# Graph layer on one core: v repeated through DRAM instead of on TensorE, and G of the next block in front of the sums over units

## The chip, the cores and the metric

One Trainium2 chip, one of its cores. The metric is device time in microseconds of one execution. The kernel before takes 751.27 us (median of 3 runs, 750.43 to 751.88).

## What is computed

A message-passing step over 53125 edges (25000 drawn pairs in both directions and 3125 loops, sorted by destination) of 3125 nodes with 32 features each (8 scalars and 8 vectors), then a layer norm. Cut to what matters:

```python
r = edge_vec / norm(edge_vec);  sh1 = SQRT3 * r
xs, xd = x[edge_src], x[edge_dst]
s1, v1 = scalars and vectors of (xs, xd)                       # 16 + 16x3 per edge
w  = relu(emb @ fc1_w1 / sqrt(10)) @ fc1_w2 / sqrt(16)         # 512 weights per edge
s_t, v_t = a1 * (sums over the 16 units of s1, v1 with w)      # "the first tensor product"
w2 = relu(emb @ fc2_w1 / sqrt(10)) @ fc2_w2 / sqrt(16)         # 384 weights per edge
scal, gates, vecs = a2 * (sums over the 8 units of s_t, v_t with w2)
edge_out = concat(tanh(scal), vecs * tanh(gates)) * edge_weight
out = layernorm(x + segment_sum(edge_out, edge_dst))
```

The per-edge weights are never formed. Instead the features are multiplied by the constant second matrices (G), the product is multiplied by the hidden layer (p), and the sum over hidden units is a matmul (S1); the second tensor product is done in the same way (z, then S2).

## The kernel before

Edges go in NB = 104 blocks of 512 (four tiles of 128). Every engine has its program written out by hand as a loop over steps i; in a step each engine works on several blocks at once, and the order of the calls in a step is the order in its queue. Semaphores with counts tie the engines; each result waits for the one that it needs and for the reader of what it overwrites. PSUM is one tensor `ps` of eight banks, shared as the code fixes it.

The stages of a block m, with the function and the line of the profile:

- GpSimd gathers the source rows (L362), TensorE turns the destinations' places into one-hot matrices (`spread_places` L921, `spread_edges` L937) and picks the destination rows out of a window (`rows` L1007). ScalarE copies all of them to SBUF. GpSimd multiplies by the directions (L404, L405), VectorE sums along them (`sum_along` L764), TensorE transposes the features (`turn_features` L947), ScalarE copies them (f, L483).
- G: `first_layer` (L1039), four f32 products (eight passes) into banks 0 to 3. `hidden_1` (L1026) gives the first hidden layer in bank 5; ScalarE applies relu (h1, L523).
- p: `products` on VectorE (L732), p_s = banks 0 to 3 times h1, 128 x 2048.
- S1: `sum_1` (L959), the sum over units of p_s into bank 7: v. ScalarE copies v to bf16 (`part_of_v` L517), TensorE takes that copy off in PSUM by the matrices `less` (`less_part` L966), and so twice more: v ends as three bf16 parts. `repeat` (L995) spreads the parts by `rep_m` over all 128 partitions into banks 0 to 3.
- z: `products2` (L770), banks 0 to 3 times the second hidden layer (h2, relu on ScalarE L529, from `hidden_2` L1032 in bank 6), 128 x 2048. S2: `sum_2` (L977) into bank 5. ScalarE copies it (u, L489), TensorE transposes u (`turn` L1019) into bank 7.
- VectorE: `gates` (L781, L784, L786) read the transposed u, then `gate_sums` (L790, L793), tanh on ScalarE (L471), `gated` (L752), `outputs` (L757). TensorE sums over nodes with the one-hot matrix (`over_nodes` L987), VectorE adds the strip of nodes into `acc` (`accumulate` L745).

On VectorE a step is: p of block i, gates of i-3, z of i-1, gated of i-4, accumulate of i-5, gate sums of i-3, outputs of i-4, sum along of i+2. SyncE's queue loads the windows, the edges' embeddings (three copies of 30 KB per block) and, every 12 blocks, the next group of embeddings. In front of the loop stands a fill that loads the inputs, splits x and the embeddings into three bf16 parts, stores these to DRAM (`x_dram`, `e_dram`) and makes the constants; behind it the last blocks are drained and the layer norm is done.

## Time and profile before

| what | us |
|---|---|
| median of the runs | 751.27 |
| profiled execution, its own time | 750.24 |
| span of the profiled execution | 748.4 |
| PE (TensorE matmul) busy | 690.1 |
| DVE (VectorE) busy | 691.3 |
| ACT (ScalarE) busy | 558.7 |
| POOL (GpSimd) busy | 529.2 |
| p, first start to last start | 38.0 to 714.7 |

The mean granted TensorE clock is 0.991 of full speed. PEld is TensorE's weight load, which overlaps its matmuls. In the chain of work that ended last, PE has 86% of the span and DVE 5%. A name such as `ps<-f,w_f` tells output and inputs of an instruction; "x4" that four rows are merged into one; `[0.19 <-PE ps L1039]` that the engine was idle for 0.19 us before it, until that one released it. The starts in a timeline are measured, the ends of matmuls modelled.

### The profile page before, as it was taken

How to read it: one execution, taken by the hardware profiler on the slowest of the kernel's cores; microseconds unless marked ns; L12 is line 12 of the kernel's file. 1: busy time of each engine (PE TensorE's matmuls, PEld its weight loads, DVE VectorE, ACT ScalarE, POOL GpSimd, SP SyncE). 2: the span in 40 equal slices, each digit the busy share in tenths (PEclk: the TensorE clock that was granted, in tenths of full speed). 3: DMA queues.
4: the chain of work that ended last, by engine and by line, in shares of the span. 5: the costliest groups of instructions: out<-in, count | busy, mean ns of one | idle time of the engine just before them, and what ended most of it. 6: DMA issues, size and time to landing. Idle time of an engine off the chain costs nothing.

```text
span 748.4 us, 19329 instructions
## 1 busy us (share of the span) xinstructions
PE 690.1 (92%) x5998; PEld 285.0 (38%) x5998; DVE 691.3 (92%) x1230; ACT 558.7 (75%) x1279; POOL 529.2 (71%) x656
## 2 busy tenths in 40 slices
PE   0578999999999999999999999999999999999963
PEld 0323434444443443444444344444444444444321
DVE  7578999999999999999999999999999999999983
ACT  2257778887788888877888888888888878788741
POOL 5678787778876887688768876888688877886100
PEclk9999999999999999999999999999999999999997
DMA  4332211121111111121112111211121111111000
GB/s 111 77 91 48 44 31 29 40 46 27 28 42 45 31 28 43 26 46 29 42 26 48 31 42 25 45 29 44 26 48 29 31 36 37 28 27 28 12 1 23
DMA packets 45714, 28.49 MB, mean 38 GB/s; under 512 B 23191, under 2 KB 43833, under 8 KB 45613
## 3 DMA queue, kind: packets, MB, share of 16 engines
q1 hardware_dynamic: 31175, 19.22, 9.8%
q0 software_dynamic: 13312, 6.84, 6.2%
q10 hardware_dynamic: 1126, 1.18, 0.6%
q8 instruction: 52, 0.85, 0.5%
q14 instruction: 49, 0.40, 0.2%
HBM read 22.46 MB, written 4.74 MB: 36 GB/s over the span
## 4 chain that ended last, share of the span: by engine, by line
PE 86%; DVE 5%; issue 2%; ACT 1%; DMA 1%; POOL 0%; DVEq 0%; ACTq 0%
PE ps L1039 15%; PE ps L959 14%; PE ps L977 13%; PE ps L966 9%; PE ps L1019 8%; PE ps L947 6%; PE ps L995 5%; PE ps L1032 4%; PE ps L1026 3%; PE ps L937 3%; DVE p_s L732 3%; PE ps L1007 3%; PE ps L921 2%; PE ps L987 2%; DVE z_s L770 1%
## 5 line engine op out<-in xcount | busy, mean ns | idle before, releaser
L362 POOL DMA_INDIRECT xs<-in_xp,src_i x416 | 401.7, 966 | 114.2 <-issue 104.1
L732 DVE TENSOR_TENSOR p_s<-ps,h 128x2048 f32<-128x2048 f32 x104 | 238.2, 2291 | 20.7 <-PE ps L1039 19.1
L770 DVE TENSOR_TENSOR z_s<-ps,h 128x2048 f32<-128x2048 f32 x104 | 237.6, 2284 | 1.0 <-PE ps L995 1.0
L517 ACT CAST v_s<-ps 128x512 bf16<-128x512 f32 x312 | 182.3, 584 | 48.7 <-PE ps L959 43.6
L1039 PE MATMUL ps<-f,w_f 32*128 32x512 f32 x832 | 120.4, 646 | 4.3
L977 PE MATMUL ps<-z_s,w_z 128*32 128x512 f32 x832 | 110.8, 605 | 2.5 <-DVE z_s L770 2.5
L959 PE MATMUL ps<-p_s,sum_m 128*32 128x512 f32 x832 | 111.8, 606 | 0.2
L483 ACT COPY f<-ps 128x512 f32<-128x512 f32 x104 | 60.9, 586 | 41.8 <-PE ps L947 41.8
L966 PE MATMUL ps<-v_s,less 128*128 128x512 bf16 x208 | 81.1, 390 | 2.3 <-ACT v_s L517 2.1
L1019 PEld LDWEIGHTS ps<-ident,u 128*128 128x128 f32 x416 | 43.8, 141 | 86.7 <-issue 86.7
L523 ACT ACTIVATE h<-ps 128x512 f32<-128x512 f32 x104 | 62.1, 597 | 19.7 <-PE ps L1026 12.4
L404 POOL TENSOR_TENSOR along<-fe,r 128x192 f32<-128x192 f32 x104 | 54.1, 520 | 30.7 <-ACT fe L495 29.3
L489 ACT COPY u<-ps 128x512 f32<-128x512 f32 x104 | 61.2, 588 | 12.4 <-PE ps L977 1.9
L529 ACT ACTIVATE h<-ps 128x512 f32<-128x512 f32 x104 | 62.2, 598 | 10.6 <-PE ps L1032 5.5
L1019 PE MATMUL ps<-ident,u 128*128 128x128 f32 x416 | 68.0, 286 | 0.2
L477 ACT ACTIVATE oht<-ps 126x512 bf16<-126x512 f32 x104 | 62.5, 601 | 7.5 <-PE ps L921 1.5
L947 PE MATMUL ps<-ident,fe 128*128 128x128 f32 x416 | 63.5, 276 | 2.9 <-ACT ohs L512 2.8
L921 PE MATMUL ps<-place,spread 5*126 5x512 bf16 x104 | 40.3, 387 | 16.7 <-DMA place<-place_dram 16.7
L966 PEld LDWEIGHTS ps<-v_s,less 128*128 128x128 bf16 x208 | 19.9, 96 | 89.4 <-ACT v_s L517 76.9
L405 POOL TENSOR_TENSOR fe<-fe,r 128x192 f32<-128x192 f32 x104 | 53.7, 517 | 0.0
L987 PEld LDWEIGHTS ps<-ohs,eo_all 128*32 128x32 f32 x832 | 25.3, 108 | 69.1 <-issue 66.4
L947 PEld LDWEIGHTS ps<-ident,fe 128*128 128x128 f32 x416 | 49.2, 143 | 5.7 <-issue 5.2
(129 smaller groups left out, 847.4 us busy)
## 6 DMA issues: line engine op xcount, KB each, us to landing
emb<-e_dram SPq DMA_DIRECT2D x309, 30.0 KB
xs<-in_xp,src_i POOLq DMA_INDIRECT x416
e_dram<-e_part SPq DMA_DIRECT2D x7, 360.0 KB
e_in<-in_emb SPq DMA_DIRECT2D x8, 240.0 KB, 2.9
window<-x_dram SPq DMA_DIRECT2D x104, 7.9 KB
x_dram<-eo_all SPq DMA_DIRECT2D x1, 585.9 KB
eo_all<-in_vec_t SPq DMA_DIRECT2D x1, 528.0 KB, 4.2
place_dram<-eo_all SPq DMA_DIRECT2D x1, 520.0 KB
```

Of the source, the lines that this page charges most:

```text
L362: nc.gpsimd.indirect_dma_start(xs_r[n][:, t, :], None, xp, bass.IndirectOffsetOnAxis(src_i[:, m * T + t:m * T + t + 1], axis=0)).then_inc( ...
L477: nc.scalar.activation(oht_r[m % 2][:], oht_ps, ACT.Relu).then_inc(oht_copied, 1)
L517: nc.scalar.copy(v_s[:], v_ps).then_inc(v_step, 1)
L529: nc.scalar.activation(h2_r[m % 3][:], h2_ps, ACT.Relu, scale=1.0 / math.sqrt(10.0)).then_inc(h2_ready, 1)
L732: nc.vector.tensor_tensor(p_s[:], ps[:, 0:4, :], h1_r[m % 2][:].unsqueeze(1).to_broadcast([128, 4, BE]), ALU.mult).then_inc(p_done, 1)
L770: nc.vector.tensor_tensor(z_s[:], ps[:, 0:4, :], h2_r[k % 3][:].unsqueeze(1).to_broadcast([128, 4, BE]), ALU.mult).then_inc(z_done, 1)
L947: last = nc.tensor.transpose(f_ps[:, TE * t:TE * t + TE], fe_r[m % 2][:, t].rearrange("p g c -> p (g c)"), ident[:])
L959: last = nc.tensor.matmul(v_ps[32 * g:32 * g + 32], sum_m[:].rearrange("p n c -> p (n c)"), p_s[:, g, :], start=True, stop=True)
L966: nc.tensor.matmul(v_ps, less[n][:], v_s[:], start=False, stop=True, skip_group_check=True).then_inc(s1_step, 1)
L977: last = nc.tensor.matmul(s2_ps[32 * g:32 * g + 32], w_z[:, min(g, 1), :], z_s[:, g, :], start=True, stop=True)
L1019: last = nc.tensor.transpose(ps[:, bank, TE * t:TE * t + TE], u_r[k % 2][:, TE * t:TE * t + TE], ident[:])
L1039: last = nc.tensor.matmul(ps[:, g, :], w_f[32 * g:32 * g + 32], f_r[m % 2][32 * g:32 * g + 32], start=True, stop=True)
```

## The change

The three bf16 parts of v, the matrices `less` and `rep_m` and the function `repeat` go. v is copied once, in f32 (`copy_v`), to one of two buffers; ScalarE's queue stores 32 of its 128 rows to `v_dram` (`store_v`, 64 KB), and SyncE's queue loads them 16 times over into 128 partitions x 2048 (`load_repeated`, 1.05 MB per block, two buffers). `products2` is one SCALAR_TENSOR_TENSOR, max(h2, 0) times the loaded copy, with h2 read from PSUM bank 6; ScalarE's copy of h2 goes. z, S2 and u of a block come a step later than before (z of i-2), the gates stay at i-3 and their sums move to the next step. On TensorE a step begins with G of block i+1, then S1 of block i. The embeddings have five buffers and are loaded a step earlier. The fill is in another order: xp, x_dram and the output go in stripes of 112 and 13 partitions, the parts of x come ahead of the directions and the selections, and the memset of `acc`, the late directions and constants stand in the first steps. The tail has no order of its own any more: the loop runs to NB + 4.

```diff
 TA = CA * T
 HALVES = ((0, 13), (13, NT))
+STRIPES = ((0, 112), (112, P))
+ER = 5
 SQRT3 = math.sqrt(3.0)
...
         h2_ps = ps[:, 6, :]
         v_ps = ps[:, 7, :]
         node_ps = ps[:, 6, 0:WIN]
-        oht_ps = ps[0:WIN * PARTS, 6, :]
+        oht_ps = ps[0:WIN * PARTS, 5, :]
         ohs_ps = ps[:, 4, T * D:T * D + T * WIN].rearrange("p (t m) -> p t m", t=T)
         turned_ps = ps[:, 7, :]
-        last_ps = ps[:, 0, :]
...
             def load_emb(m):
                 sp.wait_ge(e_stored, 16 * (m // SB + 1))
-                if m >= 3:
-                    sp.wait_ge(h2_done, m - 2)
+                if m >= ER:
+                    sp.wait_ge(h2_done, m - ER + 1)
                 for first in (0, 32, 64):
-                    sp.dma_start(emb_r[m % 3][first:first + PARTS * HID], e_dram[:, m * HID:m * HID + HID, :]
-                                 ).then_inc(emb_loaded[m % 3], 16)
+                    sp.dma_start(emb_r[m % ER][first:first + PARTS * HID], e_dram[:, m * HID:m * HID + HID, :]
+                                 ).then_inc(emb_loaded[m % ER], 16)
+
+            def load_repeated(k):
+                sp.wait_ge(v_stored[k % 2], 16 * (k // 2 + 1))
+                if k >= 2:
+                    sp.wait_ge(z_done, k - 1)
+                sp.dma_start(rep_r[k % 2][:], v_dram[k:k + 1].to_broadcast([16, 8, 4, BE])
+                             ).then_inc(rep_loaded[k % 2], 16)
...
-            sp.dma_start(bases[:], bases_row).then_inc(bases_loaded, 16)
             sp.dma_start(w1_s, w1).then_inc(weights_loaded, 16)
             sp.dma_start(w2a_s, w2a).then_inc(weights_loaded, 16)
-            sp.dma_start(w_z[:].rearrange("p n c -> p (n c)"), w2b).then_inc(weights_loaded, 16)
+            sp.dma_start(bases[:], bases_row).then_inc(bases_loaded, 16)
             sp.wait_ge(zeroed, 1)
             sp.dma_start(x_dram[N:N + WIN, :, :], no_rows[:]).then_inc(x_stored, 16)
             sp.wait_ge(place_step, 4)
             sp.dma_start(place_dram.rearrange("n (b e) -> b n e", b=NB), place_part).then_inc(place_stored, 16)
+            sp.wait_ge(x_part_ready, PARTS)
+            for top, bottom in STRIPES:
+                sp.dma_start(x_dram[0:N, :, :].rearrange("(p m) n c -> p m n c", p=P)[top:bottom], x_part[top:bottom]
+                             ).then_inc(x_stored, 16)
...
             for i in STEPS:
                 if i == 3:
                     sp.dma_start(xt_n[:], xt).then_inc(nodes_loaded, 16)
+                if real(i):
+                    load_repeated(i)
                 if real(i + 5) and i + 5 >= 4:
                     load_window(i + 5)
                 if i >= 1 and i % SB == 1 and i // SB + 1 < SUPERS:
                     load_super(i // SB + 1)
                 if i >= 6 and i % SB == 6 and i // SB + 1 < SUPERS:
                     store_super(i // SB + 1)
-                if real(i + 3) and i + 3 >= 3:
-                    load_emb(i + 3)
+                if real(i + 4) and i >= 0:
+                    load_emb(i + 4)
                 if i >= 0 and i % CB == 0 and CB * (i // CB + 3) < NB:
                     load_places(i // CB + 3)
 
...
+            def copy_v(m):
+                act.wait_ge(s1_done, m + 1)
+                if m >= 2:
+                    act.wait_ge(v_stored[m % 2], 16 * (m // 2))
+                nc.scalar.copy(v_r[m % 2][:], v_ps).then_inc(v_copied, 1)
+
+            def store_v(m):
+                act.wait_ge(v_copied, m + 1)
+                act.dma_start(v_dram[m].rearrange("c g e -> g c e"), v_r[m % 2][0:128:4, :]).then_inc(v_stored[m % 2], 16)
...
             for i in STEPS:
+                if i == -1:
+                    act.wait_ge(n2_ready, 2)
+                    nc.scalar.activation(nrm_t[:, TA:TILES], n2_t[:, TA:TILES], ACT.Sqrt).then_inc(norm_ready, 1)
                 if real(i):
-                    hidden_2(i)
+                    copy_v(i)
+                if real(i - 4):
+                    tanhs(i - 4)
                 if real(i):
-                    part_of_v(i, 0)
-                if real(i + 1):
-                    hidden_1(i + 1)
-                if real(i):
-                    part_of_v(i, 1)
-                if real(i + 3) and i < 2:
+                    store_v(i)
+                if real(i + 4) and i + 4 >= 1:
+                    copy_oht(i + 4)
+                if real(i + 3):
                     copy_sources(i + 3)
                 if real(i + 3):
                     copy_rows(i + 3)
-                if real(i + 3) and i >= 2:
-                    copy_sources(i + 3)
-                if real(i + 4):
+                if real(i + 4) and i + 4 >= 1:
                     copy_one_hot(i + 4)
-                if real(i + 4) and i + 4 >= 1:
-                    copy_oht(i + 4)
-                if real(i):
-                    part_of_v(i, 2)
-                if real(i - 3):
-                    tanhs(i - 3)
-                if real(i - 1):
-                    copy_u(i - 1)
+                if real(i - 2):
+                    copy_u(i - 2)
                 if real(i + 2):
                     copy_f(i + 2)
+                if real(i + 2):
+                    hidden_1(i + 2)
                 later_emb(i)
...
+            def part_of_x(n):
+                if n == 0:
+                    act.wait_ge(xt_loaded, 32)
+                else:
+                    act.wait_ge(x_rest_ready, n)
+                nc.scalar.copy(x_part[:, :, n, :], xt_s if n == 0 else x_rest).then_inc(x_part_ready, 1)
+
...
-            nc.vector.memset(acc[:], 0.0).then_inc(acc_zeroed, 1)
-            link(nc.vector.tensor_scalar(bad, place_f, float(WIN), None, ALU.is_ge))
-            link(nc.vector.scalar_tensor_tensor(out=bad, in0=place_f, scalar=0.0, in1=bad, op0=ALU.is_lt, op1=ALU.add))
-            nc.vector.tensor_reduce(ext[0:NB], bad, AX.X, ALU.add).then_inc(misfit_parts, 1)
-
-
...
+                nc.vector.memset(acc[:], 0.0).then_inc(acc_zeroed, 1)
...
                 dve.wait_ge(h1_ready, m + 1)
+                if m >= 1:
+                    dve.wait_ge(s1_done, m)
                 nc.vector.tensor_tensor(p_s[:], ps[:, 0:4, :], h1_r[m % 2][:].unsqueeze(1).to_broadcast([128, 4, BE]),
                                         ALU.mult).then_inc(p_done, 1)
...
             def products2(k):
-                dve.wait_ge(rep_done, k + 1)
-                dve.wait_ge(h2_ready, k + 1)
-                nc.vector.tensor_tensor(z_s[:], ps[:, 0:4, :], h2_r[k % 3][:].unsqueeze(1).to_broadcast([128, 4, BE]),
-                                        ALU.mult).then_inc(z_done, 1)
+                dve.wait_ge(h2_done, k + 1)
+                dve.wait_ge(rep_loaded[k % 2], 16 * (k // 2 + 1))
+                nc.vector.scalar_tensor_tensor(out=z_s[:], in0=h2_ps.unsqueeze(1).to_broadcast([128, 4, BE]), scalar=0.0,
+                                               in1=rep_r[k % 2][:], op0=ALU.max, op1=ALU.mult).then_inc(z_done, 1)
...
             for i in STEPS:
                 if real(i):
                     products(i)
+                if real(i - 4):
+                    gate_sums(i - 4)
+                if real(i - 2):
+                    products2(i - 2)
+                if real(i + 2):
+                    sum_along(i + 2)
                 if real(i - 3):
                     gates(i - 3)
-                if real(i - 1):
-                    products2(i - 1)
                 if real(i - 5):
                     base = base_of(i - 5)
+                    accumulate(i - 5, base)
                 if real(i - 4):
                     gated(i - 4)
-                if real(i - 5):
-                    accumulate(i - 5, base)
-                if real(i - 3):
-                    gate_sums(i - 3)
-                if real(i - 4):
                     outputs(i - 4)
-                if real(i + 2):
-                    sum_along(i + 2)
...
-                for step, at_step in enumerate((0, 1, 3, 4, 5, 6, 7, 8)):
+                for step, at_step in enumerate((-2, -2, 0, 0, 0, 1, 1, 1)):
...
                 if m == 0:
                     pe.wait_ge(consts_ready, 1)
-                    pe.wait_ge(rep_step, 6)
-                if m >= 3:
-                    pe.wait_ge(e_free, m - 2)
                 for g in range(4):
-                    last = nc.tensor.matmul(v_ps[32 * g:32 * g + 32], sum_m[:].rearrange("p n c -> p (n c)"), p_s[:, g, :],
+                    last = nc.tensor.matmul(v_ps[32 * g:32 * g + 32], sum_m[:].rearrange("p c n -> p (c n)"), p_s[:, g, :],
                                             start=True, stop=True)
-                last.then_inc(s1_step, 1)
-
...
+                last.then_inc(s1_done, 1)
+
+            def first_layer(m):
+                pe.wait_ge(f_copied, m + 1)
+                if m >= 1:
+                    pe.wait_ge(p_done, m)
+                for g in range(4):
+                    last = nc.tensor.matmul(ps[:, g, :], w_f[32 * g:32 * g + 32], f_r[m % 2][32 * g:32 * g + 32],
+                                            start=True, stop=True)
+                last.then_inc(g_done, 1)
...
+            def turn(k):
+                pe.wait_ge(u_ready, k + 1)
+                pe.wait_ge(v_copied, min(k + 4, NB))
+                if k + 4 > NB:
+                    pe.wait_ge(e_free, k)
+                for t in range(T):
+                    last = nc.tensor.transpose(turned_ps[:, TE * t:TE * t + TE], u_r[k % 2][:, TE * t:TE * t + TE], ident[:])
+                last.then_inc(tr_done, 1)
+
...
 
             for i in STEPS:
                 if i == -4:
-                    spread_places(0)
-                if real(i - 1):
-                    repeat(i - 1)
-                if real(i):
-                    hidden_2(i)
+                    misfits_of_all()
+                if i == -1:
+                    pe.wait_ge(weights_ready, 3)
+                if real(i + 1):
+                    first_layer(i + 1)
                 if real(i):
                     sum_1(i)
-                if real(i - 5):
-                    over_nodes(i - 5)
+                if real(i + 4):
+                    spread_places(i + 4)
+                if real(i - 3):
+                    turn(i - 3)
                 if real(i + 4):
                     spread_edges(i + 4)
                 if real(i + 3):
                     rows(i + 3)
-                if i == -4:
-                    misfits_of_all()
-                    keep_warm(8)
-                if i == -1:
-                    pe.wait_ge(weights_ready, 3)
-                    pe.wait_ge(misfits_ready, 1)
-                if real(i + 1):
-                    hidden_1(i + 1)
-                if real(i):
-                    less_part(i, 0)
-                if real(i + 1):
-                    first_layer(i + 1)
-                if real(i + 4) and i + 4 >= 1:
-                    spread_places(i + 4)
-                if real(i):
-                    less_part(i, 1)
-                if real(i - 1):
-                    sum_2(i - 1)
+                if real(i - 5):
+                    over_nodes(i - 5)
                 if real(i - 2):
-                    turn(i - 2)
+                    sum_2(i - 2)
                 if real(i + 2):
                     turn_features(i + 2)
-            keep_warm(2)
-            over_nodes(NB - 4)
-            turn(NB - 1)
+                if real(i - 1):
+                    hidden_2(i - 1)
+                if i == -2:
+                    pe.wait_ge(weights_ready, 2)
+                    pe.wait_ge(misfits_ready, 1)
+                if real(i + 2):
+                    hidden_1(i + 2)
+                if i == -4:
+                    keep_warm(8)
+                if i == NB:
+                    nodes_themselves()
             flag = pe.value_load(misfits[0:1, 0:1], min_val=0, max_val=EP)
-            over_nodes(NB - 3)
-            nodes_themselves()
-            over_nodes(NB - 2)
-            keep_warm(4)
-            over_nodes(NB - 1)
             keep_warm(4)
```

TensorE's queue, one step in the middle, before: from the repetition of block i-1 (L995) over S1 (L959) and G (L1039) to the second `less` product and S2.

```order
L995 MATMUL ps<-v_s,rep_m 128x512 x4
L1032 MATMUL ps<-emb,w_first 128x512
L959 MATMUL ps<-p_s,sum_m 32x512 x4
L987 MATMUL ps<-ohs,eo_all 32x42 x4
L937 MATMUL ps<-spread,place 128x42 x4
L1007 MATMUL ps<-window,oht 128x32 x4
L1026 MATMUL ps<-emb,w_first 128x512
L966 MATMUL ps<-v_s,less 128x512
L1039 MATMUL ps<-f,w_f 128x512 x4
L921 MATMUL ps<-place,spread 126x512
L966 MATMUL ps<-v_s,less 128x512
L977 MATMUL ps<-z_s,w_z 32x512 x4
```

After, one whole step: G (L956), S1 (L947), places (L900), the transposes of u (L966), edges (L916), rows (L926), nodes (L975), S2 (L989), features (L938), hidden layers (L1006, L999).

```order
L956 MATMUL ps<-f,w_f 128x512 x4
L947 MATMUL ps<-p_s,sum_m 32x512 x4
L900 MATMUL ps<-place,spread 126x512
L966 MATMUL ps<-ident,u 128x128 x4
L916 MATMUL ps<-spread,place 128x42 x4
L926 MATMUL ps<-window,oht 128x32 x4
L975 MATMUL ps<-ohs,eo_all 32x42 x4
L989 MATMUL ps<-z_s,w_z 32x512 x4
L938 MATMUL ps<-ident,fe 128x128 x4
L1006 MATMUL ps<-emb,w_first 128x512
L999 MATMUL ps<-emb,w_first 128x512
```

G and S1 have changed places, and the transposes of u now stand behind S1 of the same step with one product between them; in the kernel before they stand behind S2.

VectorE's queue, before: p (L732), the three operations of `gates` on the transposed u, z (L770).

```order
L732 TENSOR_TENSOR p_s<-ps,h_1 128x2048
L781 TENSOR_TENSOR m<-ps,r 128x96
L784 TENSOR_TENSOR m<-ps,r 128x256
L786 TENSOR_TENSOR m_0<-m,ps 128x96
L770 TENSOR_TENSOR z_s<-ps,h_0 128x2048
```

After, from accumulate (L747) over gated (L754), outputs (L759), p (L734) and the gate sums (L792, L795) to z (L772), sum along (L766) and gates (L783, L786):

```order
L747 TENSOR_TENSOR acc<-acc,ps 128x42
L754 TENSOR_TENSOR eo_all<-eo_all,wgt_s 128x4x16
L759 TENSOR_TENSOR eo_all<-m_0,eo_all 128x4x3x8
L734 TENSOR_TENSOR p_s<-ps,h_1 128x2048
L792 TENSOR_TENSOR m<-m 128x128
L795 TENSOR_TENSOR gsc<-m 128x64
L772 SCALAR_TENSOR_TENSOR z_s<-ps,rep 128x2048
L766 TENSOR_REDUCE fe<-along 128x4x16
L783 TENSOR_TENSOR m<-ps,r 128x96
L786 TENSOR_TENSOR m<-ps,r 128x256
L788 TENSOR_TENSOR m_0<-m,ps 128x96
```

The gates have moved from in front of z to behind sum along, and outputs stands right behind gated.

## Rows read from the trace of the kernel before

**Rows 1.** The page, part 1: busy us (share of the span) x instructions

```profile
PE 690.1 (92%) x5998; PEld 285.0 (38%) x5998; DVE 691.3 (92%) x1230; ACT 558.7 (75%) x1279; POOL 529.2 (71%) x656
```

**Rows 2.** Windows: stretch, length, busy us by engine, PEclk, DMA share, GB/s

```profile
24.00:26.50 2.50, 2.50 (x13) 2.29 (x11) 2.23 (x11) 0.00 (x0) 1.36 (x2) 1.00 0.36 115
37.50:39.00 1.50, 0.52 (x5) 0.00 (x0) 1.24 (x2) 0.00 (x0) 1.21 (x2) 1.00 0.97 382
69.00:70.50 1.50, 0.03 (x1) 0.00 (x0) 1.50 (x1) 1.49 (x5) 1.20 (x2) 1.00 0.10 15
72.50:75.50 3.00, 3.00 (x21) 1.24 (x19) 2.39 (x7) 2.23 (x6) 2.24 (x3) 0.50 0.15 43
400.00:450.00 50.00, 49.60 (x444) 20.72 (x441) 48.29 (x85) 40.48 (x94) 40.20 (x51) 1.00 0.15 34
```

**Rows 3.** Timeline, one block: start us, us, engine, line, what [idle before]

```profile
401.29 0.19 DVE L745 TENSOR_TENSOR acc<-acc,ps 128x42 f32 x1
...
401.40 0.28 DVE L790 TENSOR_TENSOR m<-m 128x128 f32<-128x128 f32 x1
...
401.72 0.23 DVE L793 TENSOR_TENSOR gsc<-m 128x64 f32<-128x64 f32 x1
401.86 0.29 DVE L757 TENSOR_TENSOR eo_all<-m,eo_all 128x96 f32<-128x96 f32 x1
...
402.03 0.36 DVE L764 TENSOR_REDUCE fe<-along 128x64 f32<-128x192 f32 x1
...
402.59 2.29 DVE L732 TENSOR_TENSOR p_s<-ps,h 128x2048 f32<-128x2048 f32 x1 [0.19 <-PE ps L1039]
...
404.98 0.39 PE L995 MATMUL ps<-v_s,rep_m 32*128 32x512 bf16 x4
...
406.81 0.58 ACT L517 CAST v_s<-ps 128x512 bf16<-128x512 f32 x1 [0.48 <-PE ps L959]
...
407.45 0.39 PE L966 MATMUL ps<-v_s,less 128*128 128x512 bf16 x1
```

**Rows 4.** Instructions of line L732 (p): duration min/median/max, first and last start

```profile
L732 DVE TENSOR_TENSOR p_s<-ps,h x104: 2229/2292/2293, 38.0 to 714.7; 128x2048 f32<-128x2048 f32 x104
```

**Rows 5.** Groups of DVE by form: busy, mean ns | idle before

```profile
L686 DVE MEMSET acc<- 128x3200 f32 x1 | 2.7, 2725 | 0.6 <-issue 0.6
L636 DVE RECIPROCAL eo_all<-eo_all 128x352 f32<-128x352 f32 x1 | 2.3, 2343 | 0.0
...
L688 DVE SCALAR_TENSOR_TENSOR eo_all<-eo_all 104x512 f32<-104x512 f32 x1 | 0.7, 692 | 0.0
```

**Rows 6.** Chain that ended last, same block: start us, us, what

```profile
401.39 1.14 PE ps L1039 x8
...
405.69 1.05 PE ps L959 x7
```

**Rows 7.** Timeline near the end: transposes and gates

```profile
721.98 0.66 PE L1019 MATMUL ps<-ident,u 128*128 128x128 f32 x4
...
722.67 0.26 DVE L781 TENSOR_TENSOR m<-ps,r 128x96 f32<-128x96 f32 x1 [1.89 <-PE ps L1019]
722.85 0.41 DVE L784 TENSOR_TENSOR m<-ps,r 128x256 f32<-128x256 f32 x1
...
723.18 0.24 DVE L786 TENSOR_TENSOR m<-m,ps 128x96 f32<-128x96 f32 x1
723.34 2.28 DVE L770 TENSOR_TENSOR z_s<-ps,h 128x2048 f32<-128x2048 f32 x1
```

**Rows 8.** Timeline of the fill, ACT's queue

```profile
27.12 2.28 ACTq L570 DMA_DIRECT2D emb<-e_dram  x3
```

**Rows 9.** DMA issues: out<-in, count, KB, us to landing

```profile
eo_all<-in_vec_t SPq DMA_DIRECT2D x1, 528.0 KB, 4.2
...
xt_n<-in_xt SPq DMA_DIRECT2D x1, 400.0 KB, 3.3
```

**Rows 10.** Timeline of the tail: the last sum over nodes

```profile
735.80 0.20 DVE L745 TENSOR_TENSOR acc<-acc,ps 128x42 f32 x1 [1.22 <-PE ps L987]
```

275 lines of the change are left out of this document (107 added, 168 removed).

## The prediction

> **What bounds the kernel now.** I read the busy shares first: PE and DVE are both busy 92% of the span, ACT 75%, POOL 71% [rows 1]. Two engines level at the top mean that a change in the order can turn either into the bound, so I went to a stretch in the middle: there PE is busy 49.60 us of 50 and DVE 48.29, at full clock, with the DMA engines at 0.15 [rows 2]. PE sets the pace, and DVE has almost no slack. One block's rows show how little: DVE's sum over `along` ends at 402.39, p of the next block (`products`) starts at 402.59, 0.2 us later [rows 3]. The period is 6.50 us: that p starts at 402.59 and the last one, 48 blocks on, at 714.7 [rows 3, 4]. The whole run of p's, from 38.0 to 714.7, takes 676.7 us [rows 4]. The profiled execution took 750.24 us, 1.0 below the median of the runs (751.27); the sum below is made against 750.24.
>
> **What leaves PE.** Two products with `less` and the repetition with `rep_m` go. One `less` product is 0.39 us, the repetition 0.39 [rows 3], so three of them are 1.17 us of a block that is 6.50 long. PE's work falls to about 5.4 us (starts overlap a little). The copies of v go from three to one and the copy of h2 goes, so ACT, at 75%, gets lighter too. PE can then no longer be the bound by its work, only by where it stands in somebody's chain.
>
> **What DVE does now.** Same instructions, another order. z is now a SCALAR_TENSOR_TENSOR from PSUM and the loaded copy. The one such f32 instruction of the trace takes 692 ns for 512 elements [rows 5]. Between a TENSOR_TENSOR of 128 elements (0.28) and p (2.29 for 2048) [rows 3] the line gives 0.68 for 512, so both kinds are equally fast and z stays at 2.29. `outputs` now stands right behind `gated`, whose result it needs. What such a wait costs is seen between the two gate sums: the second starts 0.32 after the first, which lasts 0.28 [rows 3], so 0.04 behind the end, where unlinked ones follow 0.1 before the end. That is +0.13. Today's 6.50, less the idle 0.19, plus 0.13 gives 6.44; some 0.04 of overlap comes back. DVE alone would need **6.4 us** a block. By that the change would win 0.1 us a block.
>
> **What the order on PE does.** This is the term that decides. p(i) reads PSUM banks 0 to 3; G(i+1) writes them and S1(i) (`sum_1`) reads p, so both start when p(i) ends. Now G stands in front. S1 writes bank 7, ACT copies v out of it, and the transposes of u(i-3) (`turn`) write the same bank: they wait for `v_copied`. DVE's `gates(i-3)` waits for these transposes, and p(i+1) stands behind it in DVE's queue. That closes a loop from p to p:
> p's end to PE's start, 0.10 (404.88 to 404.98) [rows 3]; G 1.14 and S1 1.05, end to end [rows 6]; S1's end to the copy 0.07 (406.74 to 406.81) and the copy 0.58; copy's end to the next matmul 0.06 [rows 3]; transposes 0.66, then 0.03 to DVE; the three operations of `gates` 0.18 + 0.33 + 0.16 = 0.67, start to start [rows 7]; acc 0.11; `gated` 0.23 + 0.04 with its wait (as the second gate sum, same size), `outputs` 0.17 to the next start, p 2.29 [rows 3]. `places` between S1 and the transposes lies beside the copy of v. The sum is **7.19 us**, and I take 7.18. With S1 in front of G it would be 7.18 - 1.14 = 6.04, under DVE's 6.4, and hidden. The stall stands on DVE in front of the first operation of `gates`: p's end, gate sums, z, sum along take about 2.95 us, the transposes end at 0.10 + 1.14 + 1.05 + 0.07 + 0.58 + 0.06 + 0.66 + 0.03 = 3.69, so some 0.7 us of idle per block. Bounds: if S1 can follow G as closely as starts do today (G's weights free earlier), 0.15 less; if each link costs 0.01 to 0.02 more, 7.3. So 7.03 to 7.3.
>
> **Other chains of a block, for cover.** The rest of PE (edges, rows, nodes, S2, features, two hidden layers) is 5.4 - 1.14 - 1.05 - 0.66 = some 2.6 us from 3.7 on and ends at about 6.5 of 7.18. ACT issues the store of v in front of the copy of `oht`, which S2 waits for. Three issues on ACT's queue took 2.28 us, 0.76 each [rows 8]: copy of v ends at 3.0, issue to 3.8, `oht` to 4.4, S2 to 5.5, f copied at 6.8. G(i+2) wants f at 7.2. Covered by 0.4 us; were the issue twice as long it would just be gone.
>
> **v through DRAM.** 64 KB stored, then 1.05 MB loaded. Nothing like the store with its load is in the trace. Loads of 400 and 528 KB landed 3.3 and 4.2 us after issue [rows 9]: along that line 1.05 MB is 7.9 us, and at the 382 GB/s of the busiest stretch [rows 2] 1.3 + 2.7 = 4 us. The store, smaller, 1.5 to 3. v is copied at 3.0 and z(i) starts at 2 x 7.18 + 0.4 = 14.8, so 11.8 us are there for issue, store, issue and load: 0.8 + 3 + 0.4 + 7.9 = 12.1 at the dear end, 7 at the cheap one. I take 8 to 9 and cost it at nothing. If this cover is gone, z waits, but only for what exceeds 11.8. By the Trainium skill (DMA: Bandwidth & Descriptors, "Anatomy of one DMA") a transfer is 2.0 us and its bytes at 436 GB/s, 4.4 us for this load; the rows' line says 7.9 and both fit; the page's fit is for GpSimd's path. The sum stays the same by either.
>
> **Fill.** The store of x goes in 112 + 13 rows, x's remainders move ahead of directions and selections, memsets leave POOL. Today both stores still drain at 0.36 of the DMA engines at 24 to 26.5 us [rows 2], the first loads of `emb` are issued at 27.12 [rows 8], p(0) starts 10.9 us later [rows 4]. x and e are 946 KB; at 382 GB/s 2.5 us instead of the 8 from 18.5 to 26.5, and the issue can come up to 5 us sooner. At most -10.5, at least -4 (e's store still has its three parts in front): I take **-8.5**. The first p to p now has, on DVE, the memset of acc 2.7, the reciprocal 2.3 [rows 5], four more direction steps and constants of some 2.8, and p and the sum 2.6: 10.4. The next two have no transposes yet; POOL's gathers pace them at about 6.1. Together 22.6.
>
> **Tail.** Today the last p ends at 717.0 and the last acc at 736.0: 19 us [rows 4, 10]. After: S1 and copy 1.9, issue, store and load some 7.5, z 2.3, S2 to transposes 2.5 (4 at half clock), gates to acc 3.5: 18 to 19. Level; -1 for the output in stripes, within 3 either way.
>
> **Sum.** 103 intervals of p: 22.6 + 100 x 7.18 = 740.6 against 676.7, +63.9. 750.24 + 63.9 - 8.5 - 1 = **804.6, so 805 us**, 7% slower. The loop's bounds move it 15 down and 12 up, fill and tail by 5.
>
> **Rivals.**
> *No stall (faster).* If G and S1 ran so much into each other that the transposes end by 2.95, DVE's 6.4 holds: 22.6 + 640 = 662.6, -14.1, and with fill and tail 727. It breaks even where the loop is 6.64, so where the pair takes 0.54 less than 2.19. For it: G uses 32 rows and S1 32 columns of the array at a time. Against: both took a full 1.1 us whatever stood behind them. 0.11.
> *The clock.* PE did next to nothing from 69.0 to 70.5, and 72.5 to 75.5 ran at a granted 0.50, 1.2 GHz, with PE busy throughout [rows 2]. After the change PE idles in two or three places of a block, some 1.8 us of 7.18. If a third of the blocks had G and S1 at half clock, each adds 2.2: +73, 878. Against: the gaps are of 0.5 to 0.7 us each, and busy stretches keep 1.00. 0.09.
> *DMA becomes the bound.* At today's small packets the engines moved 34 GB/s at 0.15, 227 in full: 1.11 MB are 4.9 us, and with today's 1.0 it is 5.9 of 7.18 if spread evenly; if some engines have a third more, 7.9, so +72, 877. At 382 GB/s it is 3.9 and no matter. 0.08. By the Trainium skill (DMA: Bandwidth & Descriptors, "Why a DMA increments its semaphore by 16 and not by 1") a transfer uses as many engines as divide its leading dimension: the store of v would sit on 4, the loads of `emb` on 3, all on the same lowest ones, which is how it could get uneven. No row here shows engines singly.
>
> **Chances.** Forecast 0.70 (785 to 825), no stall 0.11, clock 0.09, DMA 0.08, 0.02 left. A measurement tells 0.2%, 1.5 us. Faster by over 0.2% 0.12 (no stall, or half of it gone with a better fill), within 0.2% 0.02, slower 0.86. The range leaves out the faster case and the dear halves of the two others: 783 to 850.
>
> **What would show it.** Right: DVE idle 0.6 to 0.8 us in front of the first operation of `gates`, released by PE's transposes, in nearly every block; these released by ACT's copy of v; p to p 7.0 to 7.3; PE at about 75% and clock 1.00; the chain alternating PE, ACT, DVE. Wrong: idle in front of z, released by the load (DMA); G over 1.3 us (clock); or p to p near 6.4.

## The result, and the profile after

| | kernel before | changed kernel |
|---|---|---|
| median of 4 runs each, same chip | 750.91 us (750.43 to 751.88) | 943.97 us (936.64 to 951.16) |
| ratio, 95% interval | | 1.254 (1.242 to 1.266) |
| profiled execution, its own time | 750.24 | 938.11 |

Medians here and below are of all runs; ratios leave out runs more than 1.5% above the fastest of the same kernel (here the one of 951.16).

The change makes the kernel 25% slower. The prediction had the direction and most of its mechanism, and a size that is 139 us too small: 805 in a range up to 850.

The page of the changed kernel, parts 1 and 2 (of part 2 the granted clock, one digit for a fortieth of the span):

```profile
span 936.3 us, 17655 instructions
...
PE 695.5 (74%) x5362; PEld 258.1 (28%) x5362; DVE 747.1 (80%) x1217; ACT 399.5 (43%) x969; POOL 526.7 (56%) x653
...
PEclk9978889979799999899899899889997999899976
```

Against [rows 1]: PE and DVE were both at 92%, now neither is above 80%. PE issues 636 matmul instructions fewer and is still 5 us busier, since some of its time now runs at a lower clock. DVE is busy 56 us more, though the change gave it 13 instructions fewer. Its instructions last 37 us more in sum (30 more in `gated` and `outputs`, 11 in the gate sums, a little less elsewhere); the other 19 are that they overlap less at their ends. `gated` and `outputs` are taken up below. The 11 us of the gate sums lie in 14 of them, which last 0.6 to 1.2 us; 13 of these stand beside GpSimd's operations on the embeddings (L395, L398, 1.15 us), and end just behind them:

```profile
173.06 1.15 POOL L395 TENSOR_TENSOR e_rest<-e_in,e_part 120x512 f32<-120x512 f32 x1 [2.11 <-ACT e_part L549]
173.18 1.18 DVE L792 TENSOR_TENSOR m<-m 128x128 f32<-128x128 f32 x1
```

Its waits (us in total, times, longest):

```profile
PE ps L956 <- DVE p_s L734: 148.3, 99, 3.5
...
DVE m L783 <- PE ps L966: 105.0, 84, 2.5
```

DVE stands in front of the first operation of `gates` (L783), released by PE's transposes (L966), in 84 blocks: the stall that was predicted, at the place where it was predicted. One full-clock block in the middle, timeline (rows of PE, ACT, DVE, of GpSimd's two products, and of the queues that issue the store and the load of v):

```profile
447.46 0.28 DVE L792 TENSOR_TENSOR m<-m 128x128 f32<-128x128 f32 x1
...
447.69 1.14 PE L956 MATMUL ps<-f,w_f 32*128 32x512 f32 x8 [1.56 <-DVE p_s L734]
...
447.79 0.57 SPq L293 DMA_DIRECT2D rep<-v_dram  x1
447.92 2.28 DVE L772 SCALAR_TENSOR_TENSOR z_s<-ps,rep 128x2048 f32<-128x2048 f32 x1
...
448.76 1.07 PE L947 MATMUL ps<-p_s,sum_m 128*32 128x512 f32 x8
...
449.90 0.58 ACT L529 COPY v<-ps 128x512 f32<-128x512 f32 x1 [3.13 <-PE ps L947]
...
450.51 0.52 ACTq L533 DMA_DIRECT2D v_dram<-v  x1
...
450.62 0.63 PE L966 MATMUL ps<-ident,u 128*128 128x128 f32 x4 [0.44 <-ACT v L529]
...
451.29 0.26 DVE L783 TENSOR_TENSOR m<-ps,r 128x96 f32<-128x96 f32 x1 [0.81 <-PE ps L966]
...
451.80 0.24 DVE L788 TENSOR_TENSOR m<-m,ps 128x96 f32<-128x96 f32 x1
...
452.22 0.52 POOL L417 TENSOR_TENSOR along<-fe,r 128x192 f32<-128x192 f32 x1 [1.61 <-ACT fe L506]
...
452.40 0.20 DVE L747 TENSOR_TENSOR acc<-acc,ps 128x42 f32 x1 [0.36 <-issue]
452.52 0.29 DVE L754 TENSOR_TENSOR eo_all<-eo_all,wgt_s 128x64 f32<-128x64 f32 x1
452.69 0.52 POOL L418 TENSOR_TENSOR fe<-fe,r 128x192 f32<-128x192 f32 x1
452.85 0.51 DVE L759 TENSOR_TENSOR eo_all<-m,eo_all 128x96 f32<-128x96 f32 x1
...
453.24 2.28 DVE L734 TENSOR_TENSOR p_s<-ps,h 128x2048 f32<-128x2048 f32 x1
```

G at 447.69, S1 behind it, the copy of v, the transposes at 450.62, `gates` at 451.29 after 0.81 us of idle: the loop as predicted, link by link. But from 451.80 on, 1.44 us pass until p, where the prediction had 0.71. The row L747 says "issue": the profile names nothing that DVE waited for. L754 and L759 stand beside GpSimd's L417 and L418, and L759 takes 0.51 us against 0.29 [rows 3].

I measured the starts in all 94 blocks between the 6th and the 100th p of the profiled execution. Median interval, and what the prediction had:

| interval | predicted | median |
|---|---|---|
| p's end to G's start | 0.10 | 0.15 |
| G's start to the copy of v | 2.26 | 2.20 |
| copy of v | 0.58 | 0.58 |
| its end to the transposes | 0.06 | 0.15 |
| transposes' start to `gates` | 0.69 | 0.67 |
| `gates` to acc | 0.67 | 1.04 |
| acc to `gated` | 0.11 | 0.11 |
| `gated` to `outputs` | 0.27 | 0.40 |
| `outputs` to p | 0.17 | 0.39 |
| p | 2.29 | 2.28 |
| **period, blocks at full clock** | **7.18** | **8.0** |
| **period, mean of all** | 7.18 | **8.39** |

The mean is above the median because 24 of the 94 blocks take 9.49 us on average. These are the blocks in which G or S1 lasts over 1.3 us. ("Full-clock block" below means all others.) Such a full-clock block and the one behind it, windows (stretch, length, busy us by engine, granted clock, DMA share, GB/s):

```profile
445.30:453.20 7.90, 5.90 (x53) 2.23 (x52) 6.66 (x12) 3.57 (x10) 4.79 (x6) 1.00 0.69 160
453.20:462.70 9.50, 7.75 (x50) 2.40 (x48) 6.68 (x12) 3.54 (x9) 4.74 (x7) 0.67 0.72 161
```

and S1 in the second, beside 1.07 at full clock:

```profile
457.07 1.94 PE L947 MATMUL ps<-p_s,sum_m 128*32 128x512 f32 x8
```

Where the 187.9 us between the two profiled executions are: p runs from 32.8 to 899.0, 866.2 us against 676.7 [rows 4], +189.5; the fill is 5.2 shorter; the tail, 37.3 behind the last p against 33.7, is 3.6 longer.

### The profile page after: what moved, and what is told of

Its sections match the earlier page's. It is cut to its first block, busy times and chain, and to the rows that moved or that the text cites. A ratio compares the mean times of both kernels' runs of the same rounds, so it can differ in the third digit from the quotient of the medians.

```text
span 936.3 us, 17655 instructions
## 1 busy us (share of the span) xinstructions
PE 695.5 (74%) x5362; PEld 258.1 (28%) x5362; DVE 747.1 (80%) x1217; ACT 399.5 (43%) x969; POOL 526.7 (56%) x653
## 3 DMA queue, kind: packets, MB, share of 16 engines
q0 software_dynamic: 13312, 6.84, 4.9%
## 4 chain that ended last, share of the span: by engine, by line
DVE 38%; PE 32%; DMA 9%; issue 8%; ACT 6%; DVEq 2%; POOL 1%; ACTq 0%
DVE p_s L734 22%; PE ps L956 12%; PE ps L947 12%; PE ps L966 6%; ACT v L529 5%; DMA rep<-v_dram 5%; DMA v_dram<-v 4%; DVE m L786 3%; DVE z_s L772 3%; DVE eo_all L754 3%; DVE m L783 2%; DVE acc L747 2%; DVEq L740 2%; DVE m L788 1%; DVE eo_all L759 1%
## 5 line engine op out<-in xcount | busy, mean ns | idle before, releaser
L772 DVE SCALAR_TENSOR_TENSOR z_s<-ps,rep 128x2048 f32<-128x2048 f32 x104 | 237.6, 2285 | 15.3 <-DMA rep<-v_dram 10.7
L956 PE MATMUL ps<-f,w_f 32*128 32x512 f32 x832 | 136.2, 722 | 149.0 <-DVE p_s L734 148.3
L734 DVE TENSOR_TENSOR p_s<-ps,h 128x2048 f32<-128x2048 f32 x104 | 237.0, 2279 | 3.7 <-PE ps L947 3.7
L529 ACT COPY v<-ps 128x512 f32<-128x512 f32 x104 | 60.9, 585 | 344.4 <-PE ps L947 344.4
L417 POOL TENSOR_TENSOR along<-fe,r 128x192 f32<-128x192 f32 x104 | 53.6, 516 | 205.9 <-ACT fe L506 204.8
L947 PE MATMUL ps<-p_s,sum_m 128*32 128x512 f32 x832 | 134.2, 723 | 1.4 <-DVE p_s L734 1.4
L989 PE MATMUL ps<-z_s,w_z 128*32 128x512 f32 x832 | 122.2, 659 | 2.4 <-ACT oht L488 2.4
L783 DVE TENSOR_TENSOR m<-ps,r 128x96 f32<-128x96 f32 x104 | 26.6, 256 | 105.3 <-PE ps L966 105.0
L966 PE MATMUL ps<-ident,u 128*128 128x128 f32 x416 | 71.5, 299 | 43.5 <-ACT v L529 42.7
L956 PEld LDWEIGHTS ps<-f,w_f 32*128 32x128 f32 x832 | 37.8, 196 | 180.7 <-issue 166.7
L938 PE MATMUL ps<-ident,fe 128*128 128x128 f32 x416 | 70.9, 295 | 9.7 <-ACT ohs L523 9.7
L938 PEld LDWEIGHTS ps<-ident,fe 128*128 128x128 f32 x416 | 45.7, 146 | 102.6 <-issue 102.6
L966 PEld LDWEIGHTS ps<-ident,u 128*128 128x128 f32 x416 | 47.4, 150 | 79.5 <-issue 76.9
L539 ACT ACTIVATE h<-ps 128x512 f32<-128x512 f32 x104 | 62.1, 597 | 0.6 <-PE ps L999 0.5
L418 POOL TENSOR_TENSOR fe<-fe,r 128x192 f32<-128x192 f32 x104 | 53.8, 518 | 0.0
L759 DVE TENSOR_TENSOR eo_all<-m,eo_all 128x96 f32<-128x96 f32 x104 | 47.8, 459 | 3.6
L747 DVE TENSOR_TENSOR acc<-acc,ps 128x42 f32 x104 | 20.7, 199 | 36.0 <-issue 29.4
L900 PE MATMUL ps<-place,spread 5*126 5x512 bf16 x104 | 48.9, 471 | 0.4 <-ACT oht L488 0.4
```

Of the source, the lines that this page charges most:

```text
L529: nc.scalar.copy(v_r[m % 2][:], v_ps).then_inc(v_copied, 1)
L539: nc.scalar.activation(h1_r[m % 2][:], h1_ps, ACT.Relu, scale=1.0 / math.sqrt(10.0)).then_inc(h1_ready, 1)
L734: nc.vector.tensor_tensor(p_s[:], ps[:, 0:4, :], h1_r[m % 2][:].unsqueeze(1).to_broadcast([128, 4, BE]), ALU.mult).then_inc(p_done, 1)
L772: nc.vector.scalar_tensor_tensor(out=z_s[:], in0=h2_ps.unsqueeze(1).to_broadcast([128, 4, BE]), scalar=0.0, in1=rep_r[k % 2][:], op0=ALU.m ...
L938: last = nc.tensor.transpose(f_ps[:, TE * t:TE * t + TE], fe_r[m % 2][:, t].rearrange("p g c -> p (g c)"), ident[:])
L947: last = nc.tensor.matmul(v_ps[32 * g:32 * g + 32], sum_m[:].rearrange("p c n -> p (c n)"), p_s[:, g, :], start=True, stop=True)
```

## The experiments

Eighteen runs in five jobs. In two of the jobs, with eight runs, the kernel before took 750.8 and 751.2 us. In the three others, with ten runs, it took 984 to 990 on its chip, 31% more, and every variant landed between 950 and 1032 there; so of those ten only intervals inside a block are used, not totals. The changed kernel itself was never run on such a chip; with S1 first it took 0.989 of the kernel before there (0.985 to 0.994, fourth job). So the 25% is shown for the chips on which the kernel before takes 751.

### First job (kernel before: 990.1 us)

S1 first: in TensorE's step `sum_1(i)` goes in front of `first_layer(i + 1)`.

> S1 of block i stands in front of G of block i+1 again; all else as changed. Loop theory: the transposes of u no longer wait behind G, the 0.8 us of idle in front of the gates goes from nearly every block, DVE paces at about 7.2 us p to p (its own work with the slower small operations), the clock recovers because PE idles less: about 820 us. Rival, the trip of v through DRAM sets the pace: the loads land no earlier, p to p stays over 8 and the time over 900. Rival, the clock is set by PE's lighter load whatever the order: granted clock stays near 0.90.

Measured: 975.0 us (970.7 to 986.7).

Register load early:

```diff
+                if real(i - 5):
+                    base = base_of(i - 5)
                 if real(i - 2):
                     products2(i - 2)
...
                 if real(i - 5):
-                    base = base_of(i - 5)
                     accumulate(i - 5, base)
```

> The register load of the strip's first node (base_of) stands in front of z again, where DVE's sequencer can do it beside a long instruction. If it is the 0.38 us between the last operation of the gates and acc: that gap falls from 0.54 to 0.16, p to p by 0.38 in blocks at full clock, time by some 39 to about 905. Rival, the gap is a wait for the sums over nodes: nothing changes, 940.

Measured: 978.4 us (961.6 to 991.7).

Dummy matmuls (128 x 128 of `ident`): two in front of `turn`, six at the end of PE's step, behind a wait for the free bank.

> Two small matmuls on the identity in front of the transposes and six at the step's end fill PE's idle places; results unchanged. If the half clock costs what lies between 8.0 (blocks at full clock) and 8.39 us (mean): granted clock to 1.00, all blocks near 8.0, about 900 us. Rival, the slow blocks come from something else (DMA landing late): clock rises but a quarter of the blocks stays at 9 us or more, time over 930.

Measured: 1031.6 us (1025.7 to 1037.6).

v neither stored nor loaded, z formed with a constant 0.01 in place of the repeated v (so all that depends on v is left out):

> v is neither stored nor loaded; z multiplies by a constant buffer (so the second tensor product is wrong and its DMA traffic absent); copies, waits on PE and DVE order stay. Loop theory: only the 10.7 us of waits for the load and ACT's issue go, so 10 to 25 us less, about 920, warm blocks still 8.0. Rival, DMA traffic slows DVE's small operations or PE: outputs falls from 0.46 to 0.3 us and the time by 50 or more. Rival, the trip is the bound: below 850.

Measured: 1022.9 us (1021.6 to 1024.3). No expectation met, and no theory told from another: all four are above the changed kernel's 944 of the first measurement. They had been expected against 944, and whether this chip was slower or the edits bad could not be told, so the second job holds the changed kernel unedited.

### Second job (kernel before: 750.8 us)

> The changed kernel itself, unedited, as a yardstick for the chip on which the four edits before ran. If that chip only runs the changed kernel slower than the first one did (stalls of several engines at once, released by nothing that the trace names, as in sum_1 first), this comes out near 990 and like the kernel it is timed against there. If it comes out near 944 while its yardstick stays at 990, or the ratio is not 1.00, the four ratios before can't be read as ratios to the changed kernel.

Measured: 941.6 us (931.4 to 948.5), 1.250 (1.243 to 1.258) of the kernel before. So the result repeats on this chip, and it is the first job's chip that was different.

The first two edits together:

> Both edits that paid 1.6 and 2.2% alone: sum_1 in front of first_layer, base_of in front of products2. My theory (the loop p, G, S1, copy of v, transposes, gates, acc, gated, outputs, p): S1 first takes 1.1 us off the loop and DVE's own sum decides, base_of early takes another 0.3 off that sum; full-speed blocks at 6.5 to 6.7 us. Rival (stalls that hit all engines at once, wherever the order stands): about the sum of the two, 3 to 4% under the changed kernel, with the undisturbed blocks at 6.6 all the same and the rest in stalls.

(The 1.6 and 2.2% are against the kernel before on the first job's chip; they don't say what the edits save on the changed kernel.)

Measured: 871.1 us (868.3 to 872.5), ratio 1.161 (1.157 to 1.164). The idle in front of `gates` falls from 105.0 us in the changed kernel to 8.7, the time by 70 us, and a new wait stands in front of z:

```profile
DVE z_s L772 <- DMA rep<-v_dram: 78.0, 61, 3.0
```

The block is 7.76 us on average, neither my 6.5 to 6.7 nor stalls of all engines: something else became the bound.

The kernel before, with `base_of` moved behind `gated`:

> The kernel before, with base_of (load of the block's base into a register) moved to right in front of accumulate, behind gated: the place it has in the changed kernel. Theory: the load stands in DVE's own queue and costs 0.3 to 0.4 us per block when it is right in front of its use, so DVE's 6.3 us become 6.7 and the block goes from 6.50 to 6.7 or 6.8: 20 to 30 us more. Rival (the load costs nothing, and the 0.38 us in front of acc in the changed kernel is a wait for PE): within 0.5% of the kernel before. Besides, if the chip is the one of the four edits before, its absolute time tells whether the kernel before is disturbed there too: 750 to 790 if not, 900 and more if it is.

Measured: 750.2 us (749.3 to 751.8), ratio 0.9994 (0.998 to 1.001). The 20 to 30 us that the theory asks for don't come. But the trace shows that the edit moved the load in the code and not in time. It starts 0.02 us before z (median), as in the kernel before, and 2.2 us before `gated`, though `gated` now stands in front of it in the code. So the load still lay beside z, and this run says nothing of a load that has only short operations in front of it.

GpSimd's products held back:

```diff
                 pool.wait_ge(rows_final, m + 1)
+                if m >= 7:
+                    pool.wait_ge(eo_done, m - 6)
```

> The changed kernel with GpSimd's two products of a block (0.5 us each) held back until DVE's outputs of the same step are done, so that they no longer run beside gated and outputs but beside p. Theory: gated and outputs, slowed from 0.24 and 0.32 to 0.36 and 0.51 us where they overlap GpSimd's products, get back 0.3 us per block on the loop: 2 to 4% faster, p's duration unchanged. Rival (the slow-down is not GpSimd's): durations of gated and outputs stay at 0.36 and 0.51 and the time stays. If p grows beside GpSimd's products instead, the gain is given back there.

Measured: 888.7 us (886.0 to 893.0), ratio 1.185 (1.181 to 1.190), 53 us less from one wait more on an engine that is 56% busy. Groups of DVE in this run, then the same two of the changed kernel:

```profile
L736 DVE TENSOR_TENSOR p_s<-ps,h 128x2048 f32<-128x2048 f32 x104 | 237.4, 2283 | 2.8 <-PE ps L949 2.8
L761 DVE TENSOR_TENSOR eo_all<-m,eo_all 128x96 f32<-128x96 f32 x104 | 30.4, 293 | 3.6
L756 DVE TENSOR_TENSOR eo_all<-eo_all,wgt_s 128x64 f32<-128x64 f32 x104 | 22.8, 219 | 0.2 <-issue 0.2
```

```profile
L759 DVE TENSOR_TENSOR eo_all<-m,eo_all 128x96 f32<-128x96 f32 x104 | 47.8, 459 | 3.6
L754 DVE TENSOR_TENSOR eo_all<-eo_all,wgt_s 128x64 f32<-128x64 f32 x104 | 34.7, 333 | 0.2 <-issue 0.2
```

Both durations are back, and p, which now runs beside GpSimd's products, is not slowed (2283 ns). `gated` to `outputs` falls from 0.40 to 0.25, `outputs` to p from 0.39 to 0.18, the full-clock block from 7.97 to 7.63, which is 35 of the 53 us; the rest goes with the half clock, in which only 8 of 94 blocks have G or S1. That DVE's shorter operations are why there are fewer of these was not tested. In the changed kernel, `outputs` takes 0.51 on average where it overlaps GpSimd's products (75 blocks) and 0.32 elsewhere; acc, which reads PSUM and SBUF, stays at 0.20 beside them. The Trainium skill says why (SBUF — State Buffer, "SBUF: two separate sides"): a DVE operation with two SBUF inputs and a GpSimd operation that reads SBUF take one pair of ports in turn. The trace agrees in which operations suffer: `gated` and `outputs` have two SBUF inputs, and so have the gate sums, p and acc only one.

### Third job (kernel before: 751.2 us)

All three edits:

> sum_1 first, base_of early and GpSimd's products late, all three on the changed kernel. Alone on the chip where the changed kernel takes 942, the first two together gave 871 and the third 889. DVE's starts in a block then add up to some 6.4 us (p 2.20, gate sums 0.45, z 2.20, sum along 0.3, gates 0.50, acc 0.16, gated 0.11, outputs 0.25, 0.18). Theory A: the loop is all there is, and with it gone the block falls to 6.4 to 6.6 us and the time to 735 to 760. Theory B: the way of v through DRAM takes the loop's place. z already waits for the load for 78 and 54 us in those two; p to p can't be less than half of the trip (copy of v to z, two blocks), and that is about 14 us: block 7.0 to 7.3, time 790 to 825, z waiting for the load 0.5 to 0.8 us in most blocks.

Measured: 885.8 us (880.0 to 895.2), ratio 1.178 (1.169 to 1.186). This is theory B by what waits, and not by size: the block is 7.85 us on average (7.45 in the median) instead of 7.0 to 7.3. DVE's own work is down to 708.9 us, and z waits for the load more than ever:

```profile
DVE z_s L774 <- DMA rep<-v_dram: 111.8, 72, 4.5
```

It is even 15 us above the run with two edits. From the start of v's copy to z it now takes 16.4 us in the median instead of 15.8, and up to 12.2 of these lie behind the load's issue; PE waits 18.5 us for windows. Why, I did not find out.

> The changed kernel without v's way through DRAM: v is neither stored nor loaded, and z is formed with a constant, so what depends on v is left out. The edit of the fourth run, on another chip. Theory: in the changed kernel the trip is hidden (z waits 10.7 us for the load in the whole run, 14 times), so the full-speed block stays at 8.0 and the time within 1.5% of 942. Rival: 1.1 MB a block on the DMA engines slow other things (gathers, loads of emb, the engines' own instructions), then it is over 2% faster.

Measured: 953.3 us (951.4 to 957.8), ratio 1.271 (1.267 to 1.275). Within 1.5%, and on the slower side: in 45 of 94 blocks G or S1 ran at half clock, instead of 24 and 32 in the two profiles of the changed kernel. The full-clock block is 7.86 us instead of 7.97. So in the changed kernel the trip is hidden, and its 1.1 MB a block cost 0.11 us of a block at most. Why PE's clock fell more often without it stays open.

> The three edits of the run before last together with the removal of v's way through DRAM (v neither stored nor loaded, z formed with a constant: what depends on v is left out). This is the floor of the changed order. By theory B (the trip is what bounds the three edits together) it falls from about 800 to 730 to 750, a block of 6.4 to 6.5, DVE busy over 90% and the clock near 1. By theory A it is level with the three edits. If it stays above 780, something else in the order bounds, and the waits name it.

Measured: 789.8 us (787.1 to 790.0), ratio 1.050 (1.048 to 1.053). Against the three edits with the trip, 96 us less: that the trip bounds them is shown, though the 730 to 750 were missed. No block ran at half clock. The period is 6.84 in the median, not 6.4 to 6.5. The missing 0.4 to 0.5 stands in one place, between the gate sums and z, timeline of DVE:

```profile
444.81 0.28 DVE L789 TENSOR_TENSOR m<-m 128x128 f32<-128x128 f32 x1
445.13 0.22 DVE L792 TENSOR_TENSOR gsc<-m 128x64 f32<-128x64 f32 x1
445.77 2.29 DVE L769 SCALAR_TENSOR_TENSOR z_s<-ps,rep 128x2048 f32<-128x2048 f32 x1 [0.42 <-issue]
```

That is where this run has its register load. The line of `base_of` in the changed kernel, three instructions of DVE's own queue (duration min/median/max):

```profile
L740 DVEq TENSOR_LOAD <-bases x104: 300/307/1461, 82.9 to 922.9; - x104
L740 DVEq FUSED_REGOPS  x104: 183/183/206, 83.5 to 923.3; - x104
L740 DVEq SEQ_ASSERT  x104: 23/23/31, 83.7 to 923.5; - x104
```

307 + 183 + 23 = 0.51 us. In the kernel before, the three are as long. New theory: the queue runs ahead of the engine and works them off while earlier instructions still run, so beside z's 2.3 us they cost nothing (before, and with `base_of` behind `gated`), and with only short ones of 0.2 to 0.4 us in front they cost most of it (0.38 in the changed kernel, 0.51 here).

Dummy matmuls again:

> The changed kernel with eight dummy matmuls a block on PE (two in front of the transposes of u, six at the step's end), which fill its idle time; the edit of the third run, on another chip. Theory: a quarter of the blocks takes 1.4 us more because G or S1 run at half clock after PE's idle stretches; with the gaps filled the granted clock goes to 0.97 or more, no block is slow, and what is left is the 8.0 of a full-speed block, plus up to 0.1 for dummies in the way: 900 to 915. Rival: the slow blocks have another cause than PE's idling, the clock stays near 0.9 and the time at 940 or above.

Measured: 905.9 us (901.7 to 909.9), ratio 1.204 (1.200 to 1.209), inside the 900 to 915, 36 us below the unedited kernel. Page:

```profile
PE 822.2 (91%) x6962; PEld 442.8 (49%) x6962; DVE 747.7 (82%) x1217; ACT 399.2 (44%) x969; POOL 525.1 (58%) x653
...
PEclk9979999999999999999999999999999999999986
```

No block of the 94 has G or S1 at half clock, and the period is 8.08 on average, 7.97 in the median. 800 matmuls without a use (1600 instructions, since an f32 one counts as two) make the kernel faster: where PE's idle time is filled, its slow blocks are gone.

### Fourth job (kernel before: 984.5 us)

Here only intervals count.

> sum_1 in front of first_layer and nothing else; the edit of the first run, on another chip. My prediction's step: the 1.14 us of G leave the loop, and the loop is no longer the bound. DVE's own starts in a block of the changed kernel add up to 7.0 us (p 2.20, gate sums 0.45, z 2.20, sum along 0.3, gates 0.50, to acc 0.54, gated 0.11, outputs 0.38, p 0.37). Theory with the trip (v's copy to z takes 14 us or more, two blocks): 7.4 to 7.6 a block, 855 to 875 us, z waiting for the load. Rival (no trip, DVE's sum decides): 7.0, about 820.

Measured: 974.4 us (967.8 to 980.7). The transposes stand 2.31 us behind p's end instead of 3.08 (medians of the parts 0.05 + 1.13 + 0.58 + 0.55): behind the copy of v, PE is still busy with G, so by PE's starts the order is worth 0.77 us, not the 1.14 of G. Nothing of that reaches DVE on this chip: `gates` starts 4.12 us behind p's end (median), 3.75 in the changed kernel, since 0.85 us now pass from the transposes' end in the records to `gates`, and 0.04 did.

> base_of moved from right in front of accumulate to right behind products2 (z), nothing else. Theory: the register load runs while z's 2.3 us do, so the interval from the last of gates to acc falls from 0.54 to 0.16 us and nothing grows: full-speed block 7.6 instead of 8.0, fewer blocks at half clock since PE idles less, 885 to 905 us. Rival (the 0.54 is not the load): the interval stays and the time stays at 935 to 950.

Measured: 983.0 us (969.4 to 1004.7). The last of `gates` and acc, DVE's timeline:

```profile
485.42 0.24 DVE L788 TENSOR_TENSOR m<-m,ps 128x96 f32<-128x96 f32 x1
485.59 0.20 DVE L747 TENSOR_TENSOR acc<-acc,ps 128x42 f32 x1
```

0.17 us here, and 0.16 to 0.18 in 32 of the 94 blocks; the median is 0.26, where the changed kernel has 0.54 (in 23 blocks acc waits for PE, or for what the trace calls remote). Gate sums to z stay at 0.45.

> sum_1 first, GpSimd's products late, v neither stored nor loaded (z formed with a constant: what depends on v is left out), as in the run that took 789.8 us with 6.84 us a block, but base_of behind z instead of in front of it. Theory (a long instruction hides the register load): gate sums to z falls from 0.96 to 0.45, block 6.33, 735 to 740 us. Rival (the load costs its half microsecond wherever it stands): 785 to 790 as before, with the 0.5 us found somewhere behind z.

Measured: 951.7 us (947.4 to 957.3). Both intervals at once:

```profile
442.28 0.24 DVE L785 TENSOR_TENSOR m<-m,ps 128x96 f32<-128x96 f32 x1
442.44 0.19 DVE L745 TENSOR_TENSOR acc<-acc,ps 128x42 f32 x1
...
445.18 0.28 DVE L789 TENSOR_TENSOR m<-m 128x128 f32<-128x128 f32 x1
445.49 0.23 DVE L792 TENSOR_TENSOR gsc<-m 128x64 f32<-128x64 f32 x1
445.63 2.28 DVE L769 SCALAR_TENSOR_TENSOR z_s<-ps,rep 128x2048 f32<-128x2048 f32 x1
```

0.16 to acc, 0.45 to z (0.16 and 0.46 in the medians of the 94 blocks): behind z the load costs nothing in either place. That bears out the new theory by intervals. Neither the total of 735 to 740 us nor the block of 6.33 that it promises was seen: the shortest block of this run takes 7.92 us.

z and all that follows it a block later, three copies of `rep`, the three other edits with it:

> The whole computation: sum_1 first, base_of behind z, GpSimd's products late, and z with all that follows it one block later, with three copies of rep, so that v's way through DRAM has three blocks (19 us at 6.4) instead of two. Theory (the trip's latency of about 14 us is what bounds, not the bytes): z hardly waits for the load, the block is 6.4 to 6.6 and the time 740 to 765, about level with the kernel before (751). Rival (the DMA engines: they are busy for 0.62 of a block of 8.39 us, so 5.2 us, 0.8 of a block of 6.4, and transfers then slow each other): z still waits for the load, block over 6.8, 780 or more.

Measured: 983.0 us (976.3 to 992.4). z waits 0.3 us for the load in the whole run. But the block is 8.9 us here, so this doesn't show that three blocks of 6.4 would be enough; by the trip's 14 us in the other runs they should be, which is an estimate.

What the chips of these jobs do differently, in this job's run without the trip (timeline, ACT and DVE behind PE's transposes, which end at 144.63):

```profile
143.97 0.66 PE L964 MATMUL ps<-ident,u 128*128 128x128 f32 x4
...
144.97 0.28 PE L973 MATMUL ps<-ohs,eo_all 128*32 128x42 f32 x8
...
146.68 0.60 ACT L488 ACTIVATE oht<-ps 126x512 bf16<-126x512 f32 x1 [3.10 <-remote]
146.74 0.26 DVE L780 TENSOR_TENSOR m<-ps,r 128x96 f32<-128x96 f32 x1 [2.15 <-remote]
```

By the records (in which the ends of matmuls are modelled) PE's work is done, and what waits for it starts 2 us later, on both engines at once. On the chips where the kernel before takes 751 us the profiles show no such waits beyond a single one. What it is stays open.

### Fifth job (kernel before: 989.0 us)

> sum_1 in front of first_layer and nothing else, for a chip where the kernel before takes 751. Theory: G's 1.1 us leave the loop, DVE's own starts (7.0 us a block) and v's way through DRAM (14 us and more for two blocks) come next: 7.4 to 7.6 a block, 855 to 880 us, some 70 less than the changed kernel's 942, z waiting for the load. Rival (no trip, DVE's sum decides): 7.0, about 820.

Measured: 974.9 us (970.1 to 980.0). z waits 7.6 us for the load, in four blocks.

> z and all that follows it one block later, three copies of rep, sum_1 first, base_of behind z, GpSimd's products late, for a chip where the kernel before takes 751. On the other chip z waited 0.3 us for the load in the whole run, so the trip is no longer in the way. Theory: DVE's sum decides, 6.35 to 6.6 us a block, 740 to 770 us. Rival (the DMA engines are then busy over 0.8 of the time and slow transfers and gathers): over 6.8 a block, 780 or more, with new waits for loads of emb, window or xs.

Measured: 984.0 us (975.1 to 989.4). z waits 2.0 us for the load, once. The same kind of chip again. Neither question got its total: the price of the order of G and S1 alone, and whether z a block later reaches the kernel before. Nothing here shows a version that beats 751 us; the best whole computation took 871.

## Why the prediction missed

Its step "What the order on PE does" is right in mechanism: the loop closes over the copy of v and the transposes, and DVE stalls in front of `gates` (median 0.81 us, predicted 0.7). Opening the loop, with the register load moved too, takes this wait away and 70 us, until the trip bounds; G and S1 exchanged alone got no total on such a chip. From p's end to the start of `gates` the step has 3.69 us, and 3.75 were measured. Its last third, `gates` to p's start, is what failed: 1.22 us there, 1.94 measured. The second fault is that half clock stood among the rivals and at nothing in the sum. Period 8.39 instead of 7.18 (the terms as written add up to 7.20), so 1.21 us, 121 us over 100 blocks:

- **`gates` to acc, 0.37 of it.** The 0.67 for three operations and the 0.11 for acc were read from the end of the run [rows 7] and from a block in which acc follows `gated` [rows 3]; that the register load stands between them now, and stood behind z before, I did not see, though the part on the change has the move. Shown by the intervals of the runs with the load in front of z (0.51 there, none in front of acc) and behind it (none in either place).
- **`gated` and `outputs`, 0.35.** I took 0.27 and 0.17 from [rows 3], where DVE has them at another time of the block than GpSimd has its products. The change pushes them together. Shown by holding GpSimd back: the two intervals fall to 0.25 and 0.18, the time by 53 us, 35 of them in full-clock blocks.
- **The handovers, 0.14 slower and 0.09 faster**, the bound of 0.01 to 0.02 a link that I gave (7.3) was nearly right for the part that it covered.
- **The clock, 0.4.** I had it as a rival at 0.09, against it that the gaps were of 0.5 to 0.7 us each. They are not: PE waits 1.5 us for p in front of G (148.3 us, 99 times) and 0.4 for the copy of v in front of the transposes (42.7 us, 101 times), and one block in four has G or S1 at half clock. A third of the blocks at +2.2 us was too dear, a quarter at +1.5 is what came: the rival came on top of the forecast, not in its place. My chances treated the cases as excluding each other. Shown by the dummy matmuls, 36 us less and no such block.
- **The first three intervals** took 27.4 instead of 22.6.

*v through DRAM* at nothing: right in the changed kernel, 10.7 us of waits in all. But the working behind it does not hold. Rows of the trip in the changed kernel: store issued at 450.51 above, and over the 94 blocks 5.4 us (median) from there to the issue of the load; from that to z 7.5 where z waits. So 12.9 us from the end of v's copy, and 14.1 in the blocks where z waits, since the store is slow there (in the run with two edits 6.6 and 7.9; 14.9 where z waits). My two ends were 7 and 12.1, and the cover 11.8. The store was the dear part: for its issue and itself I had 3.8 at most. The load's 7.5 is near the 7.9 of the rows' line, and not near the 4 of the cheap end or the 4.4 that the prediction quotes. At my own period of 7.18, z would have waited; it was hidden only because the block came out longer. It bounds both runs that opened the loop.

*DVE alone 6.4 us*: 6.84 was measured with the loop open and the trip gone, of which 0.51 is the register load; 6.33 without it, an estimate from the intervals that no run's block showed.

*With S1 in front of G the loop is 6.04 and hidden*: hidden yes (8.7 us of waits in front of `gates` in the run with two edits), but PE then does G before the transposes.

*Fill −8.5, tail −1*: −5.2 and +3.6. The first load of `emb` is issued at 18.11 instead of 27.12, 9 us sooner, but then features wait for GpSimd's gathers, and G(0) takes 2.09 us at half clock. In the tail z waits for the last repeated v, with nothing left to cover it:

```profile
913.98 2.29 DVE L772 SCALAR_TENSOR_TENSOR z_s<-ps,rep 128x2048 f32<-128x2048 f32 x1 [2.82 <-DMA rep<-v_dram]
```

v's copy ended at 903.04, so 10.9 us where the step had 7.5.

Of the rivals, "no stall" and "DMA becomes the bound" did not come.

## What to carry to other kernels

When a change slides a group of instructions along an engine's queue, look at both its neighbours in the queue (the register load here was hidden beside an instruction of 2.3 us and cost 0.38 to 0.51 us behind ones of 0.2 to 0.4) and at what the other engine on the same ports does at the new time. An engine that stops being the bound starts to idle, and on PE idling had a price of its own, 36 us of 942 here: add it to the forecast instead of setting it against it. And a latency that is hidden by 12 us of cover has to be priced again whenever the period that makes the cover is what the next edit shortens.

## What the runs showed of the hardware that I had not expected

- Eight dummy matmuls a block, 800 in all, made the kernel 36 us faster (942 to 906). PE's waits before had been of 1.5 and 0.4 us.
- Operations of DVE of 0.22 and 0.29 us with both inputs in SBUF become 0.36 and 0.51 beside GpSimd's products of 0.52, and one of 0.28 becomes 1.18 beside an operation of 1.15; p of 2.28 beside the products stays at 2.28.
- The register load in DVE's queue begins before instructions that stand in front of it in the code: 0.02 us before z and 2.2 before `gated`.
- A store of 64 KB and the load of 1 MB behind it take 13 us from the store's issue to the start of what waits for the load, 5.4 of them before the load is issued.
- On the chips of three of the five jobs the same kernel takes 984 to 990 us instead of 751, and the cause stays open. A ratio is worth nothing before its yardstick has been looked at.
